# Attention with a mixture of experts: second maxima ahead of a value product, maxima negated once, ScalarE's rounds written out

## The chip, the cores and the metric

The kernel runs on one core of a Trainium2 chip. The time is device microseconds of one execution, from the runs' median. The profile is of one further execution, taken by the hardware profiler. TensorE is PE in its rows (PEld its weight loads), VectorE DVE, ScalarE ACT, GpSimd POOL, SyncE SP.

## The reference

A pre-norm transformer layer on x of 2048 tokens by 512: attention with 32 query heads and 8 key and value heads of 16 features, and then a layer of 8 experts, of which each token takes two.

```python
x = x + attention(layernorm(x))      # softmax(Q K^T / 4) V, then @ Wo + bo
h = layernorm(x)
top_vals, top_idx = top_k(h @ gate_w.T, 2)
w = softmax(top_vals)
x = x + sum over the two experts of w * (h @ expert_w[e].T + expert_b[e])
```

The change lies in the attention.

## The kernel before

The attention runs in N = 32 rounds. A round is one key head (G = 8) and one block of 512 queries (NC = 4), for the REP = 4 query heads that share that key head. It goes over the 2048 keys in NKT = 16 steps of 128 keys. Each step has UNITS / NKT = 4 score units, one per head: a matmul (`score_unit`, L1061) writes a bank of 128 keys by 512 queries, ScalarE takes the Exp of it into `probs` (L892), and a value product (`value_product`, L1071) multiplies the values with it into bank 6, in two halves of 256 queries. The value product runs BEHIND = 2 steps after its scores, so a round's last two value products come in steps 0 and 1 of the next round, and step 2 (the third step) has the first value product of the round, `values(0)`. It overwrites bank 6, so it waits until ScalarE has copied the round before out of it (`copy_outputs`, L869, semaphore `o_ready`). ScalarE does that copy just before the Exp of unit 7.

Softmax needs a shift: the maximum of the scores of each query. The maxima of a later round are found beside the scores of this one. In each step there are two maxima units (`max_unit`, L1032, each a pair of matmuls into two of the banks 2 to 5), and VectorE reduces each (L1381). At the end of step MAX_T = 10 the collected maxima are turned by TensorE (`max_transpose`, L1042), ScalarE reads them out negated (`negate_maxima`, L875 and L877), GpSimd makes the lower part of the split number (`shift_lo`, L573), and SP writes both parts into two extra rows of the queries (`place_shift`, L688). The next round's first score waits for that.

TensorE's order within a step is written out in `attention_step`: maxima unit, two scores, half a value product; maxima unit, two scores, the other half. I call each such group of three a half-step; a round has 32. The two matmuls of a pair run side by side on different rows of the array.

The scores share three banks, SBANKS = [0, 1, 7], in a ring. RING lists its entries: 64 scores, with ("maxima", 0) ahead of score 44, and a further entry ("none", 0) three later, so that the maxima keep their bank for two turns and the 66 entries are a multiple of three. Thus each score of every round has a bank of its own, and ScalarE's rounds 1 to 30 can be a loop (`act.Fori`, L896) whose waits come from a register. Rounds 0 and 31 are written out. `ring_bank_free` names what a score waits for: the Exp three entries back, or the read of the maxima (`max_read`). VectorE's rounds 1 to 29 are a loop as well; TensorE's are written out.

Of the kernel before, what the change touches and what calls it, by code (L numbers as in the profile page):

```python
# [6 lines left out]
ACT = mybir.ActivationFunctionType  # L7
# [6 lines left out]
P = 128  # L14
EPS = 1e-5

def preln_attention_moe(nc, x, Wq, bq, Wk, bk, Wv, bv, Wo, bo, gate_w, expert_w, expert_b, out):
# [6 lines left out]
    REP = D // KVD  # L24
    KD = D // P
    CH = 512
    NC = T // CH
    TT = CH // P
    NKT = T // P
    NKC = T // CH  # L30
    N = G * NC
# [5 lines left out]
    ROWS = CROW + 2  # L37
# [12 lines left out]
    BEHIND = 2  # L50

    SPLIT, MAX_T = 9, 10
    PRING = 16
    UNITS = NKT * REP

    SBANKS = [0, 1, 7]
    RING = [("score", u) for u in range(UNITS)]

    RING.insert(REP * (MAX_T + 1), ("maxima", 0))
    RING.insert(REP * (MAX_T + 1) + len(SBANKS), ("none", 0))  # L60
    assert len(RING) % len(SBANKS) == 0
    MUNITS = REP * TT * NKC // 2
    AHEAD = MUNITS - 2 * SPLIT

# [52 lines left out]
    with ExitStack() as ctx:  # L117
        def sb(name, shape, dt=F32):
            return ctx.enter_context(nc.sbuf_tensor(name, shape, dt))
# [8 lines left out]
        def sem(name):  # L128
            return ctx.enter_context(nc.semaphore(name))

        bank = ctx.enter_context(nc.psum_tensor("bank", [P, 8, CH], F32))
# [8 lines left out]
        ident = sb("ident", [P, P])  # L140
# [21 lines left out]
        max_q = sb("max_q", [P, REP * TT])  # L162
# [40 lines left out]
        negated = negated_sb[:, :]  # L203
# [56 lines left out]
        def key_slot(g):  # L260

            return (g + 1) % KSLOTS
# [7 lines left out]
        probs = arena_p[:, :].rearrange("p (r s) -> p r s", r=PRING)  # L270
# [38 lines left out]
        mT_full = sem("mT_full")  # L309
        neg_hi = sem("neg_hi")  # L310
        max_read = sem("max_read")
# [78 lines left out]
        sp_passed = sem("sp_passed")  # L390
        dve_passed = sem("dve_passed")

        def ring_bank(entry):
            return SBANKS[RING.index(entry) % len(SBANKS)]

        B_MAX = ring_bank(("maxima", 0))


        WO_BANKS, LG_BANK, RK_BANK, XT_BANK = (2, 3, 0, 1), 4, 5, 6
# [43 lines left out]
        def _(pool):  # L443
# [126 lines left out]

            def shift_lo(j):
                pool.wait_ge(max_read, j)
                pool.tensor_tensor(shift[:, 1, :], negated, shift[:, 0, :].bitcast(F32), ALU.subtract).then_inc(neg_ready, 1)  # L573

            def residual(c):
# [234 lines left out]
        def _(act):  # L810
# [23 lines left out]
            def evacuate_projection(p):  # L834

                u = PROJ[p][1]
                act.wait_ge(proj_full, p + 1)
                bias = bk_sb[:, 0:1] if u == 0 else bq_sb[:, u - 1:u]
                act.activation(qf[:, u, :], bank[:, PROJ_BANK[p], :], ACT.Identity, bias=bias).then_inc(proj_evac, 1)  # L839
                act.wait_ge(proj_evac, p + 1)  # L840
                act.activation(parts[:, u, 0, :], qf[:, u, :], ACT.Copy).then_inc(hi_ready, 1)  # L841
# [23 lines left out]
            def copy_outputs(i):  # L865

                act.wait_ge(pv_done, PRING // REP + NKT * i)
                act.wait_ge(o_lo, 1 + i)
                act.activation(o_acc[:, :], bank[:, 6, :], ACT.Copy).then_inc(o_ready, 1)  # L869

            def negate_maxima(j):
                maxima = bank[0:REP * TT, B_MAX, 0:P]
                act.wait_ge(mT_full, j + 1)
                act.wait_ge(shift_dma, 1 + 64 * j)
                act.activation(shift[:, 0, :], maxima, ACT.Copy, scale=-1.0).then_inc(neg_hi, 1)  # L875
                act.wait_ge(neg_hi, j)
                act.activation(negated, maxima, ACT.Copy, scale=-1.0).then_inc(max_read, 1)  # L877

            def round_(i, last):
                first = isinstance(i, int) and i == 0  # L880
                for u in range(UNITS):
                    if first and u == REP + 2:
                        evacuate_projection(LAST)
                    if not first and u == REP * (BEHIND - 1) + 3:
                        copy_outputs(i)
                    if u == REP * (MAX_T + 1) and not last:
                        negate_maxima(i + 1)
                    act.wait_ge(s_full, UNITS * i + u + 1)
                    if u % REP == 0:

                        act.wait_ge(pv_done, NKT * i + u // REP + 1)
                    act.activation(probs[:, u % PRING, :], bank[:, ring_bank(("score", u)), :],  # L892
                                   ACT.Exp, scale=SCALE).then_inc(p_ready, 1)

            round_(0, False)
            with act.Fori(1, N - 1) as i:  # L896
                round_(i, False)
            round_(N - 1, True)

            copy_outputs(N)  # L900

# [62 lines left out]
        def _(pe):  # L964
# [71 lines left out]
            def max_unit(j, m):  # L1036
                max_half(j, m, 0)
                max_half(j, m, 1).then_inc(m_full, 1)

            def max_transpose(j):  # L1040
                pe.wait_ge(maxq_ready, j + 1)
                pe.transpose(bank[0:REP * TT, B_MAX, 0:P], max_q[:, :], ident[:, :]).then_inc(mT_full, 1)  # L1042

            def ring_bank_free(i, entry):

                r = RING.index(entry) - len(SBANKS)
                if RING[r][0] == "none":
                    r -= len(SBANKS)
                kind, u = RING[r]
                if r < 0:  # L1050
                    pe.wait_ge(p_ready, UNITS * i + u - UNITS + len(SBANKS) + 1)
                elif kind == "score":
                    pe.wait_ge(p_ready, len(SBANKS) + UNITS * i + u + 1)
                else:
                    pe.wait_ge(max_read, min(i, N - 2) + 1)

            def score_unit(i, u):
                kt, h = u // REP, u % REP
                ring_bank_free(i, ("score", u))
                r = HALVES[h % 2]  # L1060
                pe.matmul(bank[:, ring_bank(("score", u)), :], k_st[r:r + ROWS, key_slot(i // NC), kt * P:(kt + 1) * P],  # L1061
                          q_st[r:r + ROWS, i % SLOTS, h, :], start=True, stop=True).then_inc(s_full, 1)

            def value_product(i, kt, part):
# [24 lines left out]
            for n in range(units):  # L1089
                j, m = divmod(n, MUNITS)  # L1090
# [3 lines left out]
                if n == MUNITS + 1:  # L1094

                    done = [q for q, _ in steps[:ALONE + n * rest // units] if PROJ_BANK[q] == B_MAX]
                    pe.wait_ge(proj_evac, done[-1] + 1)
                    max_transpose(0)
                if (n + 1) * rest // units > n * rest // units:
                    p, k = steps[ALONE + n * rest // units]  # L1100
                    if n > MUNITS and k == 0 and PROJ_BANK[p] == B_MAX:
                        pe.wait_ge(neg_ready, 1 + 1)
# [79 lines left out]
            def attention_step(i, kt):  # L1182

                j, m = maximum_of(i, kt)
                with_max = j < N
                if kt == 0:
                    pe.wait_ge(shift_dma, 1 + 64 * (i + 1))
                if kt == SPLIT and with_max:
                    pe.wait_ge(q_dma, 16 * NQD * (j + 1))
                    if j % NC == 0:  # L1190
                        pe.wait_ge(kr_dma, 16 * NKD * (j // NC))

                def values(part):
                    if kt >= BEHIND:
                        if kt == BEHIND and part == 0:
                            pe.wait_ge(v_ready, i // NC + 1)
                            pe.wait_ge(proj_evac, len(PROJ))
                            pe.wait_ge(o_ready, i + 1)
                        value_product(i, kt - BEHIND, part)
                    elif i > 0:  # L1200
                        value_product(i - 1, NKT + kt - BEHIND, part)
                    elif kt == 0:
                        projection_step(LAST, part)
                    elif part == 0:
                        projection_step(LAST, 2)
                        projection_step(LAST, 3)

                if with_max:
                    max_unit(j, m)
                score_unit(i, REP * kt)  # L1210
                score_unit(i, REP * kt + 1)
                values(0)
                if with_max:
                    max_unit(j, m + 1)
                score_unit(i, REP * kt + 2)
                score_unit(i, REP * kt + 3)
                values(1)
                if kt == MAX_T and i < N - 1:
                    ring_bank_free(i, ("maxima", 0))
                    max_transpose(i + 1)  # L1220
                if i == N - 2 and kt in TURN_WO:
                    for j in range(2):
                        turn_wo(2 * TURN_WO.index(kt) + j)
                if i == N - 2 and kt in WO_GATES:
                    wo_gates(WO_GATES.index(kt))
                if i == N - 1 and kt in GATES:
                    gates_step(*GATES[kt])
# [76 lines left out]
        def _(dve):  # L1304
# [84 lines left out]
            def make_shift(j, part):  # L1389

                maxima = bank[0:REP * TT, B_MAX, 0:P]
                if part == 0:
# [348 lines left out]
```

## Time and profile before

| | |
|---|---|
| median of 3 runs | 1701.26 us (1698.30 to 1703.56) |
| the profiled execution | 1700.52 us, span 1698.7 us |
| TensorE busy | 1631.1 us (96%), 13,715 matmuls |
| VectorE busy | 1444.1 us (85%) |
| ScalarE busy | 1267.5 us (75%), 1109.7 of it in the Exps of L892 |
| chain that ended last | TensorE 89%: L1071 35%, L1032 25%, L1061 16% |

How to read it: busy time alone doesn't say what bounds the kernel, and recorded matmuls overlap. The chain gives the share of each engine in what set the end. What one round costs is read from the starts of the same instruction in the timeline. The granted clock was 1.00 in the stretches of rounds shown below.

### The profile page before, as it was taken

How to read it: one execution, taken by the hardware profiler on the slowest of the kernel's cores; microseconds unless marked ns; L12 is line 12 of the kernel's file. 1: busy time of each engine (PE TensorE's matmuls, PEld its weight loads, DVE VectorE, ACT ScalarE, POOL GpSimd, SP SyncE). 2: the span in 40 equal slices, each digit the busy share in tenths (PEclk: the TensorE clock that was granted, in tenths of full speed). 3: DMA queues.
4: the chain of work that ended last, by engine and by line, in shares of the span. 5: the costliest groups of instructions: out<-in, count | busy, mean ns of one | idle time of the engine just before them, and what ended most of it. 6: DMA issues, size and time to landing. Idle time of an engine off the chain costs nothing.

```text
span 1698.7 us, 38136 instructions
## 1 busy us (share of the span) xinstructions
PE 1631.1 (96%) x13715; PEld 793.5 (47%) x13716; DVE 1444.1 (85%) x1749; ACT 1267.5 (75%) x2383; POOL 567.0 (33%) x827
## 2 busy tenths in 40 slices
PE   6999999999999999999999999999999999977995
PEld 3633444444444444444444444444444444656784
DVE  5388999999999999999999999999999973566565
ACT  3126888888888888888888888888888887304563
POOL 3121233333333333333333333333333345453222
PEclk9999999999999999999999999999999999988998
DMA  7345344423232334332323222322233014585476
GB/s 219 98 108 120 53 107 117 95 71 82 78 86 68 96 75 90 71 93 70 84 68 92 68 68 68 95 68 68 68 95 71 18 43 150 183 298 178 154 261 223
DMA packets 87863, 179.03 MB, mean 105 GB/s; under 512 B 21247, under 2 KB 25343, under 8 KB 86961
## 3 DMA queue, kind: packets, MB, share of 16 engines
q1 hardware_dynamic: 50464, 87.22, 21.8%
q0 software_dynamic: 34624, 88.25, 16.6%
q8 instruction: 107, 1.75, 0.5%
q10 hardware_dynamic: 2640, 1.59, 0.4%
q14 instruction: 28, 0.22, 0.0%
HBM read 91.14 MB, written 86.23 MB: 104 GB/s over the span
## 4 chain that ended last, share of the span: by engine, by line
PE 89%; ACT 2%; DMA 2%; issue 2%; DVE 2%; another core or an unknown queue 1%; SPq 0%; POOL 0%; ACTq 0%; DVEq 0%; POOLq 0%
PE bank L1071 35%; PE bank L1032 25%; PE bank L1061 16%; PE bank L1240 6%; PE bank L983 5%; ACT o_acc L869 1%; PE bank L1023 1%; PE bank L1269 1%; PE bank L1283 1%; DMA xs<-slots_x 1%; DMA at_lo<-at_parts 0%; DMA y_rows<-ys,tok_i 0%; PE bank L1042 0%; DMA k_parts<-parts 0%
## 5 line engine op out<-in xcount | busy, mean ns | idle before, releaser
L1381 DVE TENSOR_REDUCE max_kc<-bank 128x1 f32<-128x1024 f32 x1024 | 1243.2, 1222 | 65.3 <-PE bank L1032 48.6
L892 ACT ACTIVATE arena_p<-bank 128x512 f32<-128x512 f32 x2048 | 1109.7, 595 | 173.4 <-PE bank L1061 137.0
L1071 PE MATMUL bank<-arena_p,v_cur 128*32 128x256 f32 x8192 | 655.2, 392 | 10.6 <-ACT o_acc L869 10.6
L1032 PE MATMUL bank<-k_st,q_st 48*128 48x512 f32 x2048 | 511.0, 496 | 0.8 <-ACT qf L839 0.8
L1061 PE MATMUL bank<-q_st,k_st 50*128 50x512 f32 x2048 | 441.3, 405 | 0.8 <-ACT arena_p L892 0.8
L1032 PEld LDWEIGHTS bank<-k_st,q_st 48*128 48x128 f32 x2048 | 190.5, 183 | 428.4 <-issue 398.7
L1061 PEld LDWEIGHTS bank<-q_st,k_st 50*128 50x128 f32 x2048 | 295.1, 185 | 31.8 <-ACT arena_p L892 17.2
L1071 PEld LDWEIGHTS bank<-arena_p,v_cur 128*32 128x32 f32 x8192 | 163.0, 108 | 297.5 <-issue 156.1
L534 POOL DMA_DIRECT2D sums<-o_acc x128 | 64.8, 513 | 342.8 <-ACT o_acc L869 337.9
L537 POOL DMA_DIRECT2D sums_rec<-sums x32 | 18.2, 570 | 212.0 <-DVE sums L1411 212.0
L983 PE MATMUL bank<-xT,arena_p 128*128 128x512 f32 x160 | 84.8, 644 | 2.1 <-ACT xT L830 2.1
L542 POOL DMA_DIRECT2D rec_b<-sums_rec x128 | 62.5, 495 | 53.6 <-DMA sums_rec<-sums 50.7
L623 POOL DMA_INDIRECT y_rows<-ys,tok_i x39 | 39.5, 1012 | 118.3 <-ACT ys L939 103.5
L939 ACT ACTIVATE ys<-bank,gate 128x512 f32<-128x512 f32 x39 | 26.8, 688 | 59.6 <-PE bank L1240 47.9
L557 POOL DMA_DIRECT2D at_parts<-o_hl x128 | 66.3, 523 | 11.3 <-POOL o_hl L553 9.8
L1650 DVE TENSOR_TENSOR x2T_lo<-bank,x2T_hi 128x512 fp32r<-128x512 f32 x39 | 26.9, 691 | 45.9 <-ACT x2T_hi L903 41.4
L498 POOL TENSOR_TENSOR parts<-qf,parts 128x512 fp32r<-128x512 f32 x20 | 25.7, 1287 | 113.0 <-ACT parts L841 113.0
L839 ACT ACTIVATE qf<-bank,bq_sb 128x512 f32<-128x512 f32 x16 | 11.0, 685 | 66.3 <-PE bank L983 64.9
L546 POOL TENSOR_TENSOR o_acc<-o_acc,rec_b 128x512 f32<-128x512 f32 x32 | 41.2, 1287 | 49.7 <-DMA rec_b<-sums_rec 49.6
L911 ACT ACTIVATE std<-mv,eps_sb 128x1 f32<-128x1 f32 x16 | 4.7, 295 | 55.1 <-DVE mv L1605 41.9
L1240 PE MATMUL bank<-we_hi,x2T_hi 128*128 x156 | 43.1, 399 | 0.0
L1240 PE MATMUL bank<-we_lo,x2T_hi 128*128 x156 | 42.8, 396 | 0.0
(205 smaller groups left out, 1017.6 us busy)
## 6 DMA issues: line engine op xcount, KB each, us to landing
slots_x<-pad_row POOLq DMA_DIRECT2D x27, 1295.0 KB, 6.0
q_st<-q_parts SPq DMA_DIRECT2D x192, 128.0 KB, 4.6
xs<-slots_x SPq DMA_DIRECT2D x39, 259.0 KB
q_parts<-parts SPq DMA_DIRECT2D x16, 512.0 KB, 3.3
we_raw<-in_L_ffn_expert_w POOLq DMA_DIRECT2D x8, 1024.0 KB, 6.4
at_parts<-o_hl POOLq DMA_DIRECT2D x128, 64.0 KB
we_his<-o_hl POOLq DMA_DIRECT2D x32, 256.0 KB, 2.4
we_hi<-we_his SPq DMA_DIRECT2D x8, 1024.0 KB
```

What stands on the lines that cost most here:

```text
L534: pool.dma_start(sums[32 * h:32 * h + 32, :], o_acc[row:row + 1, :].rearrange("o (a q) -> o a q", a=32)).then_inc(sums_dma, 16)
L542: pool.dma_start(rec_b[32 * h:32 * h + DK, :], sums_rec[h].partition_broadcast(DK)).then_inc(recb_dma, 16)
L546: pool.tensor_tensor(o_acc[:, :], o_acc[:, :], rec_b[:, :], ALU.mult).then_inc(o_norm, 1)
L557: pool.dma_start(at_parts[:, row:row + DK, qc * CH:(qc + 1) * CH].rearrange("a d q -> d a q"), o_hl[32 * h:32 * h + DK, :, :].bitcast(F32) ...
L623: pool.indirect_dma_start(y_rows, bass.IndirectOffsetOnAxis(ap=tok_i[:, s % TRING, :], axis=0), ys[:, s % SR, :], None, bounds_check=2 * T ...
L892: act.activation(probs[:, u % PRING, :], bank[:, ring_bank(("score", u)), :], ACT.Exp, scale=SCALE).then_inc(p_ready, 1)
L983: mm = pe.matmul(bank[:, PROJ_BANK[p], :], w, xT[:, c, k, :], start=(k == 0), stop=(k == KD - 1))
L1032: return pe.matmul(bank[:, 2 + 2 * (m % 2) + q, :], q_st[r:r + CROW, j % SLOTS, h, qt * P:(qt + 1) * P], k_st[r:r + CROW, key_slot(j // NC ...
L1061: pe.matmul(bank[:, ring_bank(("score", u)), :], k_st[r:r + ROWS, key_slot(i // NC), kt * P:(kt + 1) * P], q_st[r:r + ROWS, i % SLOTS, h, ...
L1071: mm = pe.matmul(bank[32 * h:32 * h + 32, 6, half], v_cur[:, kt, :], probs[:, (REP * kt + h) % PRING, half], start=(kt == 0 and part == 0) ...
L1240: mm = pe.matmul(out_, a(k), w(k), start=(first and q == 0 and k == 0), stop=(q == 2 and k == KD - 1))
L1381: dve.reduce_max(max_kc[:, m:m + 1], bank[:, 2 + 2 * (m % 2):4 + 2 * (m % 2), :].rearrange("p a s -> p (a s)"), AX.X).then_inc(m_done, 1)
```

## The change

1. In steps with kt == BEHIND (the third) of all rounds but the first, the second maxima unit is issued ahead of `values(0)`, no longer behind it.
2. The entry ("none", 0) is gone. The ring has 65 entries, so its banks shift from round to round: `ring_bank` and `maxima_bank` take the round's number. The maxima keep their bank for one turn.
3. ScalarE reads the turned maxima once (into `negated`); GpSimd makes the upper part from it with a copy, and then the lower part.
4. ScalarE's rounds are all written out, with constants in the waits.

```diff
     RING.insert(REP * (MAX_T + 1), ("maxima", 0))
-    RING.insert(REP * (MAX_T + 1) + len(SBANKS), ("none", 0))
-    assert len(RING) % len(SBANKS) == 0
...
-        def ring_bank(entry):
-            return SBANKS[RING.index(entry) % len(SBANKS)]
-
-        B_MAX = ring_bank(("maxima", 0))
+        def ring_bank(i, entry):
+            return SBANKS[(len(RING) * i + RING.index(entry)) % len(SBANKS)]
+
+
+        B_MAX = SBANKS[-1]
+
+        def maxima_bank(j):
+            return ring_bank(j - 1, ("maxima", 0)) if j > 0 else B_MAX
...
             def shift_lo(j):
                 pool.wait_ge(max_read, j)
+                pool.tensor_copy(shift[:, 0, :], negated).then_inc(neg_hi, 1)
+                pool.wait_ge(neg_hi, j)
                 pool.tensor_tensor(shift[:, 1, :], negated, shift[:, 0, :].bitcast(F32), ALU.subtract).then_inc(neg_ready, 1)
...
             def negate_maxima(j):
-                maxima = bank[0:REP * TT, B_MAX, 0:P]
                 act.wait_ge(mT_full, j + 1)
                 act.wait_ge(shift_dma, 1 + 64 * j)
-                act.activation(shift[:, 0, :], maxima, ACT.Copy, scale=-1.0).then_inc(neg_hi, 1)
-                act.wait_ge(neg_hi, j)
-                act.activation(negated, maxima, ACT.Copy, scale=-1.0).then_inc(max_read, 1)
+                act.activation(negated, bank[0:REP * TT, maxima_bank(j), 0:P], ACT.Copy, scale=-1.0).then_inc(max_read, 1)
...
-                    act.activation(probs[:, u % PRING, :], bank[:, ring_bank(("score", u)), :],
+                    act.activation(probs[:, u % PRING, :], bank[:, ring_bank(i, ("score", u)), :],
                                    ACT.Exp, scale=SCALE).then_inc(p_ready, 1)
 
             round_(0, False)
-            with act.Fori(1, N - 1) as i:
-                round_(i, False)
-            round_(N - 1, True)
+            for i in range(1, N):
+                round_(i, i == N - 1)
...
                 r = RING.index(entry) - len(SBANKS)
-                if RING[r][0] == "none":
-                    r -= len(SBANKS)
...
                 score_unit(i, REP * kt)
                 score_unit(i, REP * kt + 1)
+
+                maxima_first = i > 0 and kt == BEHIND
+                if with_max and maxima_first:
+                    max_unit(j, m + 1)
                 values(0)
-                if with_max:
+                if with_max and not maxima_first:
                     max_unit(j, m + 1)
```

## Rows read from the trace of the kernel before

**Rows 1.** The page: busy time of each engine, and the chain's shares by engine
```profile
PE 1631.1 (96%) x13715; PEld 793.5 (47%) x13716; DVE 1444.1 (85%) x1749; ACT 1267.5 (75%) x2383; POOL 567.0 (33%) x827
...
PE 89%; ACT 2%; DMA 2%; issue 2%; DVE 2%; another core or an unknown queue 1%; SPq 0%; POOL 0%; ACTq 0%; DVEq 0%; POOLq 0%
```
**Rows 2.** Timeline (start us, us, engine, line, operation, count), looped round: maxima pairs
```profile
380.01 0.50 PE L1032 MATMUL bank<-k_st,q_st 48*128 48x512 f32 x2
...
393.71 0.50 PE L1032 MATMUL bank<-k_st,q_st 48*128 48x512 f32 x2
395.35 0.50 PE L1032 MATMUL bank<-k_st,q_st 48*128 48x512 f32 x2
...
400.28 0.50 PE L1032 MATMUL bank<-k_st,q_st 48*128 48x512 f32 x2
...
415.22 0.50 PE L1032 MATMUL bank<-k_st,q_st 48*128 48x512 f32 x2
...
420.91 0.50 PE L1032 MATMUL bank<-k_st,q_st 48*128 48x512 f32 x2
```
**Rows 3.** Timeline of round 0, which is written out: maxima pairs
```profile
170.03 0.50 PE L1032 MATMUL bank<-k_st,q_st 48*128 48x512 f32 x2
...
174.38 0.50 PE L1032 MATMUL bank<-k_st,q_st 48*128 48x512 f32 x2
...
175.62 0.50 PE L1032 MATMUL bank<-k_st,q_st 48*128 48x512 f32 x2
...
184.26 0.50 PE L1032 MATMUL bank<-k_st,q_st 48*128 48x512 f32 x2
```
**Rows 4.** Timeline of a looped round: a step's first scores and their Exp
```profile
345.70 0.39 PE L1061 MATMUL bank<-q_st,k_st 50*128 50x512 f32 x2
...
346.20 0.60 ACT L892 ACTIVATE arena_p<-bank 128x512 f32<-128x512 f32 x1 [0.24 <-PE bank L1061]
```
**Rows 5.** Timeline, third step of a looped round; the first row is VectorE's
```profile
352.11 1.23 DVE L1381 TENSOR_REDUCE max_kc<-bank 128x1 f32<-128x1024 f32 x1
352.26 0.64 PE L1071 MATMUL bank<-arena_p,v_cur 128*32 128x256 f32 x8
353.04 0.60 ACT L869 ACTIVATE o_acc<-bank 128x512 f32<-128x512 f32 x1
...
353.89 0.64 PE L1071 MATMUL bank<-arena_p,v_cur 128*32 128x256 f32 x8 [0.34 <-ACT o_acc L869]
354.01 0.61 ACT L892 ACTIVATE arena_p<-bank 128x512 f32<-128x512 f32 x1
...
355.70 0.50 PE L1032 MATMUL bank<-k_st,q_st 48*128 48x512 f32 x2
```
**Rows 6.** Timeline, round 0, the step after the maxima were turned
```profile
171.77 0.25 ACT L875 ACTIVATE shift<-bank 16x128 fp32r<-16x128 f32 x1
171.81 0.63 PE L1061 MATMUL bank<-q_st,k_st 50*128 50x512 f32 x2
...
172.24 0.60 ACT L892 ACTIVATE arena_p<-bank 128x512 f32<-128x512 f32 x1
...
172.73 0.59 ACT L892 ACTIVATE arena_p<-bank 128x512 f32<-128x512 f32 x1
172.94 0.50 PE L1032 MATMUL bank<-k_st,q_st 48*128 48x512 f32 x2
...
173.28 0.60 PE L1061 MATMUL bank<-q_st,k_st 50*128 50x512 f32 x2
```
**Rows 7.** Timeline, shift of a looped round; last, the page's row of its transfers
```profile
376.70 0.44 POOL L573 TENSOR_TENSOR shift<-negated,shift 16x128 fp32r<-16x128 f32 x1 [0.91 <-ACT negated L877]
...
377.22 3.15 SPq L688 DMA_DIRECT2D q_st<-shift  x4
...
q_st<-shift SPq DMA_DIRECT2D x128, 8.0 KB, 2.4
```
**Rows 8.** The page, DMA queues: packets, MB, share of 16 engines; here TensorE's instructions
```profile
q8 instruction: 107, 1.75, 0.5%
```

More of the change, by code:

```diff
@@ L1041, in max_transpose @@
                 pe.wait_ge(maxq_ready, j + 1)
-                pe.transpose(bank[0:REP * TT, B_MAX, 0:P], max_q[:, :], ident[:, :]).then_inc(mT_full, 1)
+                pe.transpose(bank[0:REP * TT, maxima_bank(j), 0:P], max_q[:, :], ident[:, :]).then_inc(mT_full, 1)
             def ring_bank_free(i, entry):
                 r = RING.index(entry) - len(SBANKS)
-                if RING[r][0] == "none":
-                    r -= len(SBANKS)
                 kind, u = RING[r]
@@ L1060, in score_unit @@
                 r = HALVES[h % 2]
-                pe.matmul(bank[:, ring_bank(("score", u)), :], k_st[r:r + ROWS, key_slot(i // NC), kt * P:(kt + 1) * P],
+                pe.matmul(bank[:, ring_bank(i, ("score", u)), :], k_st[r:r + ROWS, key_slot(i // NC), kt * P:(kt + 1) * P],
                           q_st[r:r + ROWS, i % SLOTS, h, :], start=True, stop=True).then_inc(s_full, 1)
```

## The prediction, written before the changed kernel ran

> **What bounds the kernel now.** I read the chain of work that ended last first: TensorE carries 89% of it [rows 1], so only time on TensorE's queue counts. Then I followed the attention loop, 32 rounds of 32 half-steps (a pair of maxima matmuls L1032, a pair of scores L1061, half a value product L1071), by the starts of the L1032 pairs. In one inner round [rows 2] the intervals are: 11 half-steps in 13.70 us (380.01 to 393.71), one of 1.64, four in 4.93 (to 400.28), twelve in 14.94 (to 415.22), and four in 5.69 around the turned maxima (to 420.91): 40.90 us. Round 0, which ScalarE already runs written out, has eight in 9.88, so 1.235 each, and 5.59 for the four around its maxima [rows 3]. So an inner round has three losses: 23 plain half-steps that cost 28.64 instead of 23 x 1.235 = 28.41, about 0.40 at the third step, and about 0.7 around the maxima. VectorE isn't the bound: its reductions take 1.23 us [rows 5], and after the wait at the third step it has room.
>
> **Term 1, ScalarE's rounds written out.** In the loop, the first Exp of a step (the one that waits for a value product too) starts 0.50 us after its scores: 345.70 to 346.20 [rows 4]. The same Exp in round 0, with constants in its waits, starts 0.43 after them: 171.81 to 172.24 [rows 6]. Scores three units on wait for that Exp's bank, and TensorE's half-step grows every second time. VectorE's rounds are a loop too from round 1 on, but its reductions end well before their banks are wanted again (term 3), so I give the whole difference to ScalarE: 28.64 - 28.41 = 0.23 plus 5.69 - 5.59 = 0.10, thus 0.33 a round, x30 looped rounds = 10.0 us. The bounds are 0 (the cause is something else) and 10; I take 10, since the alternation sets in with the first looped round. The round's end lies among the eleven half-steps of 13.70 (1.245 each), the same as the twelve of 14.94 (1.245) in mid-round, so the jump back costs nothing today and removing it gives nothing.
>
> The Trainium skill (Perfetto Trace Analysis, Identifying Dependency Chains) says that an instruction that waits for several engines may get a separate wait instruction ahead of it. If that were the cost, writing the rounds out would keep it and this term would be 0; the round 0 rows, where the same Exp with the same two waits takes 0.43, speak against it here.
>
> **Term 2, one read and one turn of the ring.** In round 0 the rows show what the change meets [rows 6]. Scores 44 start at 171.81, but score 45 must wait for Exp 43, whose slot is three entries back; this stays, since the maxima still take an entry of the ring. The negations run at 171.77 and after it. Exp 44 starts at 172.24, which is 0.43 after its scores: one negation less doesn't start it earlier in a written-out round. In the second half the maxima pair is at 172.94 and scores 46 at 173.28, but score 47 has to wait for Exp 45 (172.73 + 0.59 = 173.32), because the maxima hold their bank for a second turn. That half-step lasts 172.94 to 174.38 = 1.44 us. With the new ring score 46 waits for the one negation, over by about 172.1, and score 47 for Exp 44 (ended 172.84): both are over before 173.28. So 1.44 becomes 1.235: 0.205 a round, x31 turned maxima = 6.4 us. The bounds are 0 and about 0.45 a round (all but the transpose goes: 5.59 - 4 x 1.235 = 0.65, less some 0.2); I take 0.205, as the releases are named by the ring itself. The transpose (0.2) stays.
>
> **Term 3, the third step.** Counting from the value product at T = 352.26 [rows 5]: ScalarE starts the copy o_acc at T+0.78 and the third step's value product starts at T+1.63, 0.25 after the copy's end. The moved maxima pair starts where that product would, about T+1.24. Its bank needs the reduction that began at 352.11 and takes 1.23, over at 353.34, T+1.08: free. It has 0.39 us until T+1.63, a little less than its recorded 0.50, and before the change the scores followed such a pair 0.34 later (172.94 to 173.28 [rows 6]); so it is out of the way by T+1.63, and the product doesn't come earlier. After it, at about T+2.20, scores 10 and 11 are next, without a maxima pair ahead. Here is the catch: score 11 reuses the bank of Exp 8, which starts at 354.01, T+1.75, behind the copy, and lasts 0.61: T+2.36. In round 0 a score that waited for an Exp until 173.32 was followed by the next maxima pair at 174.38, 1.06 later, with the value product between [rows 3, 6]; here that makes T+3.42. Before, this maxima pair started at 355.70 = T+3.44. So the wait for the copy becomes one for Exp 8: 0.02 a round, x30 = 0.6 us. Below it I put 0; above, the whole 1.64 - 1.235 = 0.405, x30 = 12.2 us. I take 0.6, since ScalarE's queue from copy to Exp 8 has no gap.
>
> **GpSimd.** It now makes the upper half of the shift itself: one more operation on 16x128, and one wait. The nearest row is its own subtraction of that size, 0.44 us [rows 7]. Behind it stand SP's shift transfers, then this round's weight split. SP's four issues end at 377.22 + 3.15 = 380.4, the last lands 2.4 later, 382.8; the next round's first scores come at about 393.71 - 4 x 1.245 = 388.7. Cover of 5.9 us for 0.5: nothing. Were it gone, the 0.5 would cost 15 us over all rounds. ScalarE loses one small negation, off the path as said. Round 0's maxima turn in the old bank; later rounds rotate over the same three banks, and no reader changes its wait otherwise.
>
> **The sum.** 10.0 + 6.4 + 0.6 = 17.0 us. The profiled execution took 1700.52 (span 1698.7), which gives 1683.5; the median of the runs is 0.74 above it, so 1684.3 us. What lies behind the rounds moves with them: its transfers hang on the last rounds, not on a fixed time.
>
> **Rivals.**
> *The alternation isn't ScalarE's.* Then term 1 is 0 and 7.0 remain: 1694.3 us. For it: round 0 is also a round in which VectorE's code is written out. Against: the 0.50 against 0.43 is ScalarE's own. Chance 0.13.
> *The third step is covered wholly.* If score 11 isn't held by Exp 8, term 3 is 12.2: 1672.7. For it: nothing but the claim of a free TensorE between T+1.24 and T+1.63. Against: 354.01 + 0.61. Chance 0.10 (with values between counted here).
> *Slower: ScalarE's code has to be fetched.* Written out, 30 rounds of 66 instructions, with up to two separate waits for each Exp, are 2,000 to 6,000 instructions that pass once. TensorE has 27,431 in its 107 packets of instructions [rows 1, 8], 256 to a packet; so ScalarE gets 8 to 23 packets. If ScalarE stopped for each as long as a small transfer needs to land, 2.4 us [rows 7], TensorE would stop with it, since three banks hold but 1.2 us of scores: 19 to 55 us, 1703 to 1739. It decides from eight such stops on (17.0 / 2.4 = 7). Against: TensorE passes its own packets, one every 16 us, and no stretch of the rounds shown has a stop like that. Chance 0.04.
> *The change does not do what it says:* the written-out waits and the single read leave everything within 0.3%, because TensorE finds another wait of the same size (a reduction late by a bank): 1699 to 1701. Chance 0.03.
>
> The Trainium skill (Runtime: NRT & Kernel Launch, Instruction fetch mechanics) has both sides of the fetch: crossing a block is mostly hidden, while a taken branch whose target has been left behind stalls. The first agrees with TensorE's even pace here. The second would add a gain at each of ScalarE's 30 loop ends; the 13.70 us of the stretch with the loop's end show none, so nothing is added.
>
> **How the numbers follow.** The forecast, 1684.3, has 0.70. With the first rival it makes 0.83, so the range reaches to 1694.5; below it takes in a term 2 of the upper kind by half and a part of term 3, to 1679. About 0.3% (5 us) is what a measurement can tell from no change: the forecast and the first two rivals are faster by more, 0.93; same 0.03; slower 0.04.
>
> **What would show it.** Term 1 right: L1032 pairs 1.235 apart in all plain half-steps, with no alternation, and the first Exp of a step 0.43 behind its scores. Term 2: one long half-step of some 1.47 after the transpose's own 1.44, then 1.24. Term 3: the third step's value product still about 1.63 after the one before, and the maxima pair of the fourth step 3.42 after T, with score 11 released by ScalarE rather than the copy. A round of 40.33 to 40.35 in place of 40.90. The prediction is wrong if the round is above 40.6 (term 1 fell) or under 40.1 (term 3 was worth its whole wait), or if ScalarE shows gaps that TensorE didn't cause.

## The result, and the profile after

| | before | after |
|---|---|---|
| median of the comparison, 4 runs each | 1699.78 us (1697.52 to 1703.56) | 1679.48 us (1676.17 to 1683.34) |
| ratio | | 0.9876, 95% interval 0.9855 to 0.9897 |
| profiled execution, and its span | 1700.52, 1698.7 | 1676.17, 1674.4 |
| one round (median interval between two turned maxima) | 40.90 us | 40.26 us |
| first turned maxima of the rounds at | 171.26 us | 167.55 us |
| from the last turned maxima to the end | 300.9 us | 299.7 us |

The change gained 20.3 us in the medians, 1.2%, where 17.0 were forecast. The measured median, 1679.48 us, lies 0.5 above the low end of the range (1679), and the ratio puts it 0.3 below (0.9876 x 1699.78 = 1678.7 us, with an interval from 1675 to 1682). The number alone is thus near the edge. Of the 4.8 us between 1684.3 and 1679.48, 1.5 are the median before, which the forecast took as 1701.26 from three runs; the other 3.3 are gain that wasn't forecast. The profiled execution is 24.3 us shorter, but 3.7 of these lie ahead of the first turned maxima, which no part of the change touches; another execution of the same kernel (e12 below) has this point at 173.06. The 30 intervals between the first and the last turned maxima went from 1226.5 to 1207.1 us: 19.4. In e12 they take 1208.3.

The page of after; the first two rows answer [rows 1], and the last is the queue that brings the instructions of the engines other than TensorE. It had 28 packets before and 46 now.

```profile
PE 1619.0 (97%) x13715; PEld 766.8 (46%) x13716; DVE 1439.6 (86%) x1749; ACT 1256.9 (75%) x2352; POOL 575.7 (34%) x858
...
PE 91%; DVE 2%; DMA 2%; issue 2%; ACT 2%; another core or an unknown queue 1%; SPq 0%; DVEq 0%; POOLq 0%; ACTq 0%
...
q14 instruction: 46, 0.38, 0.1%
```

The timeline of one round of after, maxima pairs (now L1033), which answers [rows 2]:

```profile
372.97 0.50 PE L1033 MATMUL bank<-k_st,q_st 48*128 48x512 f32 x2
...
386.56 0.50 PE L1033 MATMUL bank<-k_st,q_st 48*128 48x512 f32 x2
...
389.32 0.50 PE L1033 MATMUL bank<-k_st,q_st 48*128 48x512 f32 x2
...
394.27 0.50 PE L1033 MATMUL bank<-k_st,q_st 48*128 48x512 f32 x2
...
407.86 0.50 PE L1033 MATMUL bank<-k_st,q_st 48*128 48x512 f32 x2
409.30 0.50 PE L1033 MATMUL bank<-k_st,q_st 48*128 48x512 f32 x2
...
410.75 0.50 PE L1033 MATMUL bank<-k_st,q_st 48*128 48x512 f32 x2
...
411.99 0.50 PE L1033 MATMUL bank<-k_st,q_st 48*128 48x512 f32 x2
```

Eleven half-steps take 13.59 us on either side (1.235 each, no alternation). The maxima cost 1.44 and 1.45 and then 1.24. The third step lasts 2.76 (386.56 to 389.32), where the prediction had 3.42 - 0.57 = 2.85. In this execution it is the one place where the round differs from the forecast: 40.26 for 40.345. In e12 the third step is the same, and the round is 40.30 because its half-steps are about 0.001 us longer each.

The third step of after, one round earlier, which answers [rows 5] (the first row is VectorE's):

```profile
345.62 1.23 DVE L1384 TENSOR_REDUCE max_kc<-bank 128x1 f32<-128x1024 f32 x1
345.74 0.64 PE L1070 MATMUL bank<-arena_p,v_cur 128*32 128x256 f32 x8
...
346.44 0.60 ACT L874 ACTIVATE o_acc<-bank 128x512 f32<-128x512 f32 x1
...
346.90 0.50 PE L1033 MATMUL bank<-k_st,q_st 48*128 48x512 f32 x2
...
347.33 0.64 PE L1070 MATMUL bank<-arena_p,v_cur 128*32 128x256 f32 x8
347.42 0.60 ACT L894 ACTIVATE arena_p<-bank 128x512 f32<-128x512 f32 x1
...
347.90 0.67 PE L1060 MATMUL bank<-q_st,k_st 50*128 50x512 f32 x2
...
348.50 0.64 PE L1070 MATMUL bank<-arena_p,v_cur 128*32 128x256 f32 x8
...
349.07 0.50 PE L1033 MATMUL bank<-k_st,q_st 48*128 48x512 f32 x2
```

With T = 345.74: the copy starts at T+0.70, no longer at T+0.78. The moved maxima pair starts at T+1.16, 0.05 after VectorE's reduction of 345.62 is over (346.85). The value product starts at T+1.59, Exp 8 at T+1.68 and is over at T+2.28. The two scores take 0.67 together instead of the usual 0.40, as the second waits for Exp 8, and the fourth step's maxima pair comes at T+3.33.

### The profile page after: what moved, and what is told of

It is laid out like the page before. It is cut to its first block, busy times and chain, and to the rows that moved or that the text cites. A ratio compares the mean times of both kernels' runs of the same rounds, so it can differ in the third digit from the quotient of the medians.

```text
span 1674.4 us, 36095 instructions
## 1 busy us (share of the span) xinstructions
PE 1619.0 (97%) x13715; PEld 766.8 (46%) x13716; DVE 1439.6 (86%) x1749; ACT 1256.9 (75%) x2352; POOL 575.7 (34%) x858
## 3 DMA queue, kind: packets, MB, share of 16 engines
q8 instruction: 107, 1.75, 0.5%
q10 hardware_dynamic: 2640, 1.59, 0.4%
## 4 chain that ended last, share of the span: by engine, by line
PE 91%; DVE 2%; DMA 2%; issue 2%; ACT 2%; another core or an unknown queue 1%; SPq 0%; DVEq 0%; POOLq 0%; ACTq 0%
PE bank L1070 35%; PE bank L1033 26%; PE bank L1060 16%; PE bank L1243 6%; PE bank L984 5%; PE bank L1024 1%; PE bank L1272 1%; DMA xs<-slots_x 1%; DMA at_lo<-at_parts 1%; PE bank L1286 1%; DMA y_rows<-ys,tok_i 0%; PE bank L1043 0%; DVE stats L1606 0%; DMA ys<-y_rows 0%
## 5 line engine op out<-in xcount | busy, mean ns | idle before, releaser
L1033 PE MATMUL bank<-k_st,q_st 48*128 48x512 f32 x2048 | 512.0, 497 | 0.8 <-ACT qf L844 0.8
L1060 PE MATMUL bank<-q_st,k_st 50*128 50x512 f32 x2048 | 432.1, 403 | 0.8 <-ACT arena_p L894 0.8
L1033 PEld LDWEIGHTS bank<-k_st,q_st 48*128 48x128 f32 x2048 | 190.5, 183 | 422.6 <-issue 374.4
L1060 PEld LDWEIGHTS bank<-q_st,k_st 50*128 50x128 f32 x2048 | 268.0, 185 | 37.2 <-ACT arena_p L894 26.2
L1243 PE MATMUL bank<-we_hi,x2T_hi 128*128 x156 | 43.2, 399 | 0.0
```

The lines of the kernel that those rows point to most:

```text
L1033: return pe.matmul(bank[:, 2 + 2 * (m % 2) + q, :], q_st[r:r + CROW, j % SLOTS, h, qt * P:(qt + 1) * P], k_st[r:r + CROW, key_slot(j // NC ...
L1060: pe.matmul(bank[:, ring_bank(i, ("score", u)), :], k_st[r:r + ROWS, key_slot(i // NC), kt * P:(kt + 1) * P], q_st[r:r + ROWS, i % SLOTS, ...
L1243: mm = pe.matmul(out_, a(k), w(k), start=(first and q == 0 and k == 0), stop=(q == 2 and k == KD - 1))
```

## The experiments

Two questions. What makes the half-steps alternate between 1.23 and 1.26 us? A: the register in ScalarE's waits; B: VectorE's loop; E: the loop itself; G: any further instruction. And where do the unforecast 0.09 us of the third step come from? A: the copy's wait held a register too; C: the moved maxima pair. D asks whether the gain at the turned maxima came from the single read. F came up on the way and is told at e8. The round is the median interval between two turned maxima in the profiled execution. The same kernel gave 40.26 and 40.30 in two executions, so a difference of 0.04 says nothing by itself; the positions inside a step agree within 0.01. Runs e5, e6, e9, e11 and e13 rest on a single execution each. T is the start of the value product ahead of the copy.

| | round, us | third step: copy, product, next maxima pair after T | ratio to before |
|---|---|---|---|
| before | 40.90 | 0.78, 1.63, 3.44 | |
| after; e12, the same again | 40.26; 40.30 | 0.70, 1.59, 3.33 | 0.9876; 0.9895 (0.9862 to 0.9928) |
| e1 ScalarE written out alone | 40.49 | 0.71, 1.56, 3.37 | 0.9925 (0.9902 to 0.9948) |
| e2 VectorE written out alone | 40.93 | as before | 1.0009 (0.9998 to 1.0020) |
| e3 after, old third step | 40.30 | 0.70, 1.56, 3.36 | 0.9890 (0.9867 to 0.9914) |
| e4 after, two turns of the ring | 40.45 | as after | 0.9913 (0.9887 to 0.9939) |
| e5 after, two reads | 40.30 | as after | |
| e6 before, the copy as last wait | 40.87 | 0.79, 1.53, 3.41 | |
| e8 after, copy behind Exp 7 and as last wait | 40.34 | 1.08, 1.82, 3.39 | 0.9899 (0.9865 to 0.9934) |
| e9 before, two rounds a turn of the loop | 40.87, every second 42.5 to 54.5 | 0.78 and 0.71 by turns (e9 below) | |
| e10 after, old third step, copy as last wait | 40.25 | 0.71, 1.45, 3.33 | 0.9897 (0.9864 to 0.9930) |
| e11 after, pair moved in three steps | 40.51 | as after | |
| e13 after, two more waits for each Exp | 40.30 | as after | |

**e1, ScalarE written out alone.**

```diff
-            with act.Fori(1, N - 1) as i:
-                round_(i, False)
-            round_(N - 1, True)
+            for i in range(1, N):
+                round_(i, i == N - 1)
```

> The kernel before with one edit: ScalarE's rounds 1 to 30 are written out, so its waits hold constants. The ring of 66, the two reads and the order of the third step stay. Theory A (a register in a ScalarE wait delays what waits by some 0.08 us, the first Exp of a step and the copy o_acc alike): the maxima pairs stand 1.235 us apart in all plain half-steps, and the copy starts 0.70 after the value product before it instead of 0.78. An inner round is 40.90 - 0.33 - 0.08 = 40.48 us, the whole 12.5 us shorter. Rival B (the alternation comes from VectorE's loop): 40.90, no change. Rival C (the 3 us that the change gained beyond the forecast belong to the moved maxima pair): 40.57 here, the copy still at 0.78, 10 us shorter.

Measured: 40.49 us a round, and by the ratio 12.7 us off the median of that chip (0.9925 x 1688.98). The third step of e1, in the old order:

```profile
391.12 0.64 PE L1070 MATMUL bank<-arena_p,v_cur 128*32 128x256 f32 x8
...
391.83 0.60 ACT L869 ACTIVATE o_acc<-bank 128x512 f32<-128x512 f32 x1
...
392.68 0.64 PE L1070 MATMUL bank<-arena_p,v_cur 128*32 128x256 f32 x8 [0.25 <-ACT o_acc L869]
...
394.49 0.50 PE L1031 MATMUL bank<-k_st,q_st 48*128 48x512 f32 x2
```

The copy starts 0.71 after the product and the fourth step's pair 3.37 after it, against 0.78 and 3.44 in [rows 5]. Theory A has both sizes; B and C don't.

But the register in a wait is not enough by itself. All four Exps of a looped step wait against a register, and only the first is late. The third of a looped step of before, with its scores:

```profile
344.45 0.42 PE L1061 MATMUL bank<-q_st,k_st 50*128 50x512 f32 x2
...
344.88 0.60 ACT L892 ACTIVATE arena_p<-bank 128x512 f32<-128x512 f32 x1
```

It starts 0.43 after its scores, as in round 0. The first Exp of a step and the copy have two waits each. Before each of them stands a register instruction that makes the value for the second wait. In the trace that instruction holds the first wait, the one that ends last: for the Exp of [rows 4] it starts at 346.1, 0.4 after the scores, and the Exp 0.08 after it. Written out there is no register instruction, and the wait that ends last stands on the Exp or the copy itself. Theory A is therefore right in size, and is better put as: a register instruction stands between the wait that matters and what it releases. e9 shows the same for the copy.

**e2, VectorE written out alone.** The edit is the same for its rounds 1 to 29.

> The kernel before with one edit: VectorE's rounds 1 to 29 are written out instead. Theory A: 40.90 us a round, no change in the time beyond 2 us. Rival B: the alternation of 1.23 and 1.26 is gone, 40.57 a round, 10 us shorter.

Measured: 40.93 us and the alternation still there, for instance 1.23, 1.26, 1.23, 1.26 from 383.66 on. B falls.

**e3, the old third step in the changed kernel.**

```diff
-                maxima_first = i > 0 and kt == BEHIND
+                maxima_first = False
```

> The changed kernel with one part undone: in the third step the second maxima pair stands behind the first half of the value product again. Theory A: Exp 8 behind the copy holds score 11 either way, so the move is worth next to nothing: product at T+1.55 (T the value product before; copy at T+0.70, 0.60 long, 0.25 until TensorE moves), maxima pair of the fourth step at T+3.36 instead of T+3.33; round 40.28 against 40.255 us, the whole 1 us longer. Rival C (the moved pair brought the unforecast 0.09): round 40.34 to 40.37, 3 us longer.

Measured: pair of the fourth step at T+3.36, 0.03 later than in after, round 40.30. By the positions the move brings 0.03 us a round, 1 us in all, which the medians can't tell from nothing. C falls.

**e4, two turns of the ring.**

```diff
+    RING.insert(REP * (MAX_T + 1) + len(SBANKS), ("none", 0))
...
+                if RING[r][0] == "none":
+                    r -= len(SBANKS)
```

> The changed kernel with one part undone: the ring has its none entry again (66 entries), so the maxima keep their bank for two turns and score 47 waits for Exp 45; one read by ScalarE and the written-out rounds stay. Theory A: the second half-step after the turn is 1.44 us again, round 40.46 against 40.255, the whole 6.3 us longer. Rival D (the gain at the turned maxima came from the single read, not the ring): round 40.255, nothing longer.

Measured: the half-steps at the turned maxima are 1.44, 1.45 and 1.45, where after has 1.44, 1.45 and 1.24. Round 40.45. The second turn costs 0.2 us in that half-step, as in the second term.

**e5, two reads.** ScalarE makes the upper part again, GpSimd only subtracts.

```diff
-                pool.tensor_copy(shift[:, 0, :], negated).then_inc(neg_hi, 1)
-                pool.wait_ge(neg_hi, j)
...
+                act.activation(shift[:, 0, :], maxima, ACT.Copy, scale=-1.0).then_inc(neg_hi, 1)
+                act.wait_ge(neg_hi, j)
+                act.activation(negated, maxima, ACT.Copy, scale=-1.0).then_inc(max_read, 1)
```

> The changed kernel with one part undone: ScalarE reads the turned maxima twice again (it makes both the upper part and the negated maxima), GpSimd only subtracts. The one-turn ring stays. Theory A: Exp 44 can't start before its scores plus 0.43 anyway and the maxima's release has over 0.8 us of room, so the round stays at 40.255 us, within 0.02. Rival D (the single read matters): 40.30 to 40.55, since a second read of 0.28 us stands ahead of Exp 44.

Measured: 1.45, 1.46 and 1.23 at the maxima, round 40.30, which is e12's. The expectation of 40.255 within 0.02 was missed, and was narrower than what two executions of one kernel differ by; the half-steps at the maxima decide, and they don't move. D falls: the single read is worth nothing here.

**e9, two rounds in a turn of the loop.**

```diff
-            with act.Fori(1, N - 1) as i:
-                round_(i, False)
+            with act.Fori(0, (N - 2) // 2) as q:
+                round_(2 * q + 1, False)
+                round_(2 * q + 2, False)
```

> The kernel before with ScalarE's loop over 15 turns of two rounds each; waits still come from a register, loop ends are halved. Theory A (the register in the waits is the cost): 40.90 us a round, half-steps still alternate between 1.23 and 1.26 in both rounds of a turn, the copy 0.78 after the value product. Rival E (the cost is the loop itself, its end or its fetching): a part of the 0.41 us is gone, 40.5 to 40.8.

Measured: 1796.02 us, 94 us slower than before, which neither theory expected. Rounds without a loop's end take 40.87 us (the first 40.75), with the alternation in both rounds of a turn: halving the loop ends gives nothing back, and E falls. The copy is where A's expectation failed. It starts 0.78 after the product in the first round of a turn and 0.71 in the second, though both are looped:

```profile
183.79 0.64 PE L1072 MATMUL bank<-arena_p,v_cur 128*32 128x256 f32 x8
184.57 0.60 ACT L869 ACTIVATE o_acc<-bank 128x512 f32<-128x512 f32 x1
L868 ACTq ALU_OP  x1: 35/35/35, 184.5 to 184.5; - x1
...
224.70 0.64 PE L1072 MATMUL bank<-arena_p,v_cur 128*32 128x256 f32 x8
225.40 0.60 ACT L869 ACTIVATE o_acc<-bank 128x512 f32<-128x512 f32 x1
L868 ACTq EVENT_SEMAPHORE  x1: 17/17/17, 224.9 to 224.9; - x1
```

The rows of L868 tell the instruction that stands ahead of the copy, its ns and its start. In the first round it is a register instruction (ALU_OP), which starts only when the product is done, and the copy comes 0.08 after it. In the second it is a plain wait (EVENT_SEMAPHORE) for the other semaphore, done half a microsecond earlier, and the copy itself waits for the product.

The rounds with a loop's end take 42.5 to 54.5. One loop end, timeline of e9:

```profile
353.43 0.40 PE L1062 MATMUL bank<-q_st,k_st 50*128 50x512 f32 x1
354.93 2.06 ACT L892 ACTIVATE arena_p<-bank 128x512 f32<-128x512 f32 x4 [2.46 <-issue]
355.58 0.49 PE L1062 MATMUL bank<-q_st,k_st 50*128 50x512 f32 x1 [1.75 <-ACT arena_p L892]
```

ScalarE stands 2.46 us with nothing to wait for ("issue"), and TensorE 1.75 for it. At the 14 loop ends ScalarE stood 1.7 to 2.6 us. At another one, where it stood 2.27 us until 264.02, the stop was followed by this; the columns are the stretch, its length, busy us of PE, PEld, DVE, ACT and POOL, the granted clock, the DMA share and GB/s:

```profile
240.00:260.00 20.00, 20.00 (x193) 8.72 (x192) 18.91 (x17) 17.20 (x34) 9.72 (x13) 1.00 0.63 176
261.00:264.00 3.00, 2.11 (x20) 0.80 (x15) 2.96 (x3) 0.75 (x2) 0.00 (x0) 1.00 0.09 19
264.00:284.00 20.00, 19.33 (x117) 6.39 (x117) 10.51 (x10) 11.61 (x22) 2.06 (x4) 0.57 0.27 41
284.00:300.00 16.00, 16.00 (x152) 7.17 (x148) 15.28 (x15) 14.26 (x28) 9.69 (x15) 1.00 0.24 68
```

TensorE was idle for 0.9 of 3 us, then the granted clock was 0.57 for 20 us, mostly its lower level of 1.2 GHz, and the half-steps were 2.16 us instead of 1.24. That interval between turned maxima was 49.85 us, so one stop of 2.3 us cost 9.0. The clock fell after 11 of the 14 loop ends, for 3 to 27 us. After the other three, the one of 354.93 among them, it stayed at 1.00, and the interval was 42.5 to 43.2. ScalarE's code has to come by the instruction queue: 99 packets in e9, 28 before, 46 in after.

```profile
q14 instruction: 99, 0.81, 0.2%
```

The Trainium skill (Runtime: NRT & Kernel Launch, Instruction fetch mechanics) says that a taken branch whose target isn't in the window of two pages forces a fetch before execution goes on. The traces agree so far as they go: a turn with two rounds stops at each jump back and brings more packets, one with a single round doesn't. Its other sentence, that crossing a block is mostly hidden, agrees with the changed kernel, where 18 more packets cost no stop.

**e13, two more waits for each Exp.**

```diff
                     act.wait_ge(s_full, UNITS * i + u + 1)
+                    if i > 0:
+                        act.wait_ge(consts, 6)
+                        act.wait_ge(b_dma, 32)
```

> The changed kernel with two further waits ahead of every Exp of rounds 1 to 31, both against constants and long satisfied, so ScalarE has two more instructions for each Exp and nothing that it really waits for. Theory A (it is the register's instruction, of which the loop had about one for each Exp, that delays the wait): round 40.25 to 40.30, half-steps 1.235 apart, Exp 0.43 behind its scores. Rival G (any further instruction between two Exps costs the same 0.08): the first Exps of a step start 0.5 or more behind their scores again, the alternation is back, round 40.5 or more.

Measured: 1,984 more instructions in the trace (38,079 against 36,095), half-steps of 1.24, copy at T+0.70, pair at T+3.32, round 40.30. So the number of instructions isn't the cost, and G falls as it was put. Before had 2,041 more than after, and lost 0.33 + 0.08 us a round. But the added waits don't stand where the register instructions stood: for the Exp of 345.32, whose scores come at 344.90, they are done by 344.3, and the Exp itself waits for its scores. What a constant wait would cost between the wait that matters and the Exp is not shown for ScalarE; the next run asks it of TensorE.

**e6, the copy as TensorE's last wait, in the kernel before.**

```diff
                     pe.wait_ge(p_ready, len(SBANKS) + UNITS * i + REP * (kt + 1))
+                if part == 0 and kt == 0:
+                    pe.wait_ge(o_ready, i + 1)
...
-                            pe.wait_ge(o_ready, i + 1)
```

> The kernel before with two waits of TensorE swapped at the first value product of a round: it waits for the probabilities (long there) first, and for the copy o_acc last. Asked: whether the 0.25 us from the copy's end to the product come from a further wait that stands behind it, and whether Exp 8 is what binds next. If so, the product starts 0.06 to 0.10 after the copy's end, 0.15 to 0.19 earlier than before, but score 11 then waits for Exp 8 (over at T+2.36), so the round gains less than the product does: 40.75 to 40.87 us. If Exp 8 doesn't bind, the whole 0.15 to 0.19 shows: 40.70 to 40.75. If the lag belongs to the copy itself, nothing moves.

```profile
393.06 0.64 PE L1073 MATMUL bank<-arena_p,v_cur 128*32 128x256 f32 x8
...
393.85 0.60 ACT L869 ACTIVATE o_acc<-bank 128x512 f32<-128x512 f32 x1
...
394.59 0.64 PE L1073 MATMUL bank<-arena_p,v_cur 128*32 128x256 f32 x8 [0.23 <-ACT o_acc L869]
...
395.50 0.48 PE L1061 MATMUL bank<-q_st,k_st 50*128 50x512 f32 x2
```

Measured: the product starts 0.14 after the copy's end (393.85 + 0.60 = 394.45) instead of 0.25, so the wait behind it cost 0.11, less than the 0.15 to 0.19 I expected. The next score pair takes 0.48 instead of 0.40, held by Exp 8, and only 0.03 of the 0.10 that the product gained arrives at the fourth step.

**e8, the copy behind Exp 7 and as last wait.** The edit of e6 in the changed kernel, and `u == REP * BEHIND` for the copy's place.

> The changed kernel with ScalarE's copy o_acc behind Exp 7 instead of ahead of it, and the copy as TensorE's last wait at the first value product. By theory A what binds the third step is Exp 8 behind a copy that itself waits 0.1 us for the last value product. Behind Exp 7 the copy finds its product ready: Exp 7 at T+0.59, copy 1.08 to 1.68, value product at 1.74 to 1.78, scores 10 and 11 at 2.31 with Exp 8 over at 2.17, maxima pair of the fourth step at T+3.21 to 3.25 instead of 3.33. Round 40.14 to 40.18 against 40.255, 2.5 to 3.5 us shorter than the changed kernel. If the late copy costs more than it gives: 40.3 or more.

```profile
390.45 0.64 PE L1072 MATMUL bank<-arena_p,v_cur 128*32 128x256 f32 x8
...
392.84 0.50 PE L1060 MATMUL bank<-q_st,k_st 50*128 50x512 f32 x2
393.27 0.64 PE L1072 MATMUL bank<-arena_p,v_cur 128*32 128x256 f32 x8
393.84 0.51 PE L1033 MATMUL bank<-k_st,q_st 48*128 48x512 f32 x2
```

Measured: pair at T+3.39, not 3.21 to 3.25, round 40.34. The product came at T+1.82, 0.04 to 0.08 late. The rest I had not seen: both scores start at once (0.50, with Exp 8 over 0.22 before them), yet the next product comes 0.43 after them, where score pairs usually leave after 0.33. These scores stand alone between two products. This is theory F: pairs that stand together overlap, and a pair alone costs 0.1 more. e11 tests it.

**e11, the pair moved in three steps.**

```diff
-                maxima_first = i > 0 and kt == BEHIND
+                maxima_first = i > 0 and kt in (BEHIND, 4, 6)
```

> The changed kernel with the second maxima pair ahead of the value product in steps 4 and 6 too, where no copy is waited for. Theory F: each of these steps is 0.1 us longer, as the score pair is then alone between two value products; round 40.42 to 40.50. If a moved pair costs nothing in itself: 40.255.

Step 4 of e11, where no copy is waited for:

```profile
396.40 0.50 PE L1033 MATMUL bank<-k_st,q_st 48*128 48x512 f32 x2
396.73 0.40 PE L1060 MATMUL bank<-q_st,k_st 50*128 50x512 f32 x2
396.99 0.49 PE L1033 MATMUL bank<-k_st,q_st 48*128 48x512 f32 x2
397.41 0.64 PE L1070 MATMUL bank<-arena_p,v_cur 128*32 128x256 f32 x8
397.98 0.49 PE L1060 MATMUL bank<-q_st,k_st 50*128 50x512 f32 x2
398.40 0.64 PE L1070 MATMUL bank<-arena_p,v_cur 128*32 128x256 f32 x8
398.97 0.50 PE L1033 MATMUL bank<-k_st,q_st 48*128 48x512 f32 x2
```

The step lasts 2.57 us (396.40 to 398.97) instead of 2.47. Three pairs together take 1.01 (396.40 to 397.41), one alone 0.42 (397.98 to 398.40): 1.43, where two and two take 2 x 0.67. Step 6 lasts 2.59, and the round 40.51, 0.21 over e12. F holds: moving the pair costs 0.1 us a step by itself, which in the third step is hidden under the copy.

**e10, the old third step with the copy as last wait; e12, the changed kernel on the same chip.**

> The changed kernel with the third step's old order (the second maxima pair behind the first half of the value product), and with the copy as TensorE's last wait at that product. Theory F (a maxima pair moved together with two others leaves the next pair alone between two value products, and a pair alone costs 0.43 where two together cost 0.67, so the move itself costs 0.1; the wait behind the copy costs 0.11): product at T+1.44, maxima pair at T+2.01, scores at T+2.35 with Exp 8 over at T+2.28, next maxima pair at T+3.25 instead of T+3.33 in the changed kernel. Round 40.18 to 40.20, 2 us shorter than the changed kernel. If Exp 8 alone binds (theory A's reading), scores 11 is late all the same and the round stays 40.25 or more.

> The changed kernel itself, on the same chip as the next two. Both theories: round 40.255 us, first turned maxima wherever the start-up puts them (167 to 171 us, it varies from run to run), the whole 1.1 to 1.3% under the kernel before.

```profile
386.93 0.64 PE L1072 MATMUL bank<-arena_p,v_cur 128*32 128x256 f32 x8
...
388.38 0.64 PE L1072 MATMUL bank<-arena_p,v_cur 128*32 128x256 f32 x8
...
389.28 0.48 PE L1060 MATMUL bank<-q_st,k_st 50*128 50x512 f32 x2
...
390.26 0.50 PE L1033 MATMUL bank<-k_st,q_st 48*128 48x512 f32 x2
```

Measured for e10: product at T+1.45 as expected, but the pair at T+3.33, not 3.25: the scores took 0.48 again, since Exp 8 (over at T+2.28) came a little too late for a score at T+2.35. Ratio 0.9897 against e12's 0.9895, no difference. So the third step ends at T+3.33 either way, with the pair moved or with the product 0.14 earlier: Exp 8 behind the copy sets it. (With neither, e3, it is T+3.36.) No version here beats the changed kernel.

Measured for e12: round 40.30, 0.04 over the 40.255 expected; first turned maxima at 173.06, outside the 167 to 171 expected; ratio 0.9895, as expected.

## Why the prediction was off

**Term 1** (0.33 us a round, 10.0 in all) was right in size and place. The eleven plain half-steps take 13.59 as written, and e1, e2 and e9 leave ScalarE's looped waits as the only cause tried that stands. The cause was named too widely: a wait against a register costs nothing by itself (the third Exp of a looped step, 0.43). The 0.08 is lost where a register instruction comes between the wait that ends last and what it releases. That is close to the rule that the prediction argued against, an instruction ahead that holds a wait. Written out, waits still stand ahead of these instructions (e13 has more of them), but they are done early and cost nothing.

**Term 2** (0.205) was right: 1.24 in place of 1.44, and 0.2 comes back with the second turn (e4). The single read adds nothing (e5).

**Term 3** (0.02 a round, measured 0.11) named the right next bound, Exp 8, but was mis-sized. The failed step is "ScalarE starts the copy o_acc at T+0.78". This I read off a looped round and kept, although term 1 had just taken 0.07 to 0.08 from the first Exp of each step, and the copy has two waits like that Exp. Written out it starts at T+0.70, Exp 8 is over at T+2.28 instead of T+2.36, and the pair forecast for T+3.42 comes at T+3.33. In e1, where only the loop is gone, this alone moves the pair by 0.07 (3.44 to 3.37); the move of the maxima pair brings the other 0.03 (e3), for the 0.02 forecast. 0.09 x 30 = 2.7 us, about the gap of 2.6 between the 16.8 forecast for the 30 intervals and the 19.4 measured. With e12's intervals the gap is 1.4, so its size in whole microseconds is known to about 1 us, and the shift in the step to 0.01. The remaining 0.7 of the 3.3 us that the median gained beyond the forecast isn't located; executions of one kernel differ by more.

**A step that held by luck:** I took the moved pair to be "out of the way by T+1.63". It starts only when VectorE's reduction is over (346.85) and TensorE leaves it 0.43 later, at 347.33, just when the product could start anyway. And I had no price for standing alone, the 0.1 of e11; the copy hides it.

**The rivals.** VectorE's loop fell (e2). The third step is not covered wholly. The slow rival's mechanism was real but in the other place: written out, ScalarE's code came in 18 more packets (8 to 23 were estimated) and none stopped it; it is the jump back over two rounds that stops it (e9). Bodies between these two sizes and above were not tried. GpSimd's copy took 0.28 us and stayed covered.

The range's low end, 1679, allowed for a larger term 2 and a part of term 3, not for a coupling of terms; by the ratio the time came out 0.3 under it.

## What to carry to other kernels

When one part of a change makes an engine's waits quicker, re-time every other wait of that engine before costing the other parts from the old trace. Where an instruction in a loop has two waits, see which of them ends last, and whether a register instruction stands behind it. Ahead of writing a loop out, look for the same code outside the loop in the same trace: here round 0 gave the gain to 0.01 us a half-step. And a loop whose body is longer can stop at its jump; check for "issue" ahead of the first instruction after the jump.

## What the runs showed of the hardware

- A register instruction of ScalarE between the wait that ended last and what it released cost 0.07 to 0.08 us (0.50 against 0.43 after the scores, 0.78 against 0.70 after the value product). A looped wait without one there cost nothing (the third Exp of a step, 0.43; the copy in e9's second rounds, 0.71), and neither did two further waits against constants that were over early (e13).
- A loop body of one round (67 activations and their waits) jumped back without a gap; one of two rounds stopped ScalarE for 1.7 to 2.6 us at its end, and rounds with such an end were 1.6 to 13.6 us longer.
- In e9, TensorE was idle 0.9 us between 261 and 264, and its granted clock averaged 0.57 over the next 20 us. After the stop ending at 354.93, with a wait of 1.75 us, it stayed at 1.00.
- Pairs of 48- and 50-row matmuls between two value products: one pair 0.42 to 0.43 us, two pairs 0.67, three 1.01.
- A further wait behind the one that matters cost TensorE 0.11 us at the value product, though it was long satisfied: 0.25 against 0.14 after the copy's end.
- The start-up of one and the same kernel differed by 5.5 us between two executions (167.55 and 173.06 at the first turned maxima).
